# q's product in the last layer's PSUM bank, beside k's in one step

## The chip, the core and the metric

The kernel runs on one core of a Trainium2 chip. Its time is in device microseconds; below it stands as the median of three runs. TensorE does the matmuls, ScalarE and VectorE read their results out of PSUM (GpSimd does the small arithmetic on rows in SBUF), and SyncE issues most DMAs. PSUM is used in eight banks of 128 partitions by 512 fp32.

## The reference

Eight batches of 512 tokens with 128 features go through three residual layers, each on a layer norm of its input:

```python
x = x + 0.5 * ffn(layernorm(x))      # "pre": fc1 128->512, silu, fc2 512->128, residual inside
x = x + attn(layernorm(x))           # 16 heads of 8
x = x + 0.5 * ffn(layernorm(x))      # "post": the same weights as "pre"
```

In the attention, `q, k, v = split(x @ w_qkv)`, `w = relu(q k^T / sqrt(8))`, each row of `w` is divided by its sum plus 1e-6, `out = w v`, then `y = x + out @ w_out + b_out` and a layer norm with gamma and beta. Everything is fp32; the ffn's weights are dequantised in the kernel.

## The kernel before

The attention of a batch b sets the beat. It goes in 16 steps (four groups of four heads, by four tiles of 128 keys). In each step TensorE computes four score products of 512 queries (`step_scores`, line 831, one bank each), ScalarE takes the relu of two of them and VectorE of the other two (lines 1135 and 1408; in some steps ScalarE takes three), and TensorE then computes the values with the probabilities of the step before (`step_values`, line 854, eight matmuls). The scores of a step can be written only when the relus of the step before are done, since the four score banks are single.

All other matmuls are written by hand into gaps of these steps. The lists `PE_START` (batch 0), `PE_SECOND` (batch 1), `PE_ORDER` (batches 2 to 5), `PE_BARE` (batch 6) and `PE_END` (batch 7) name for each step what comes before and behind the values; `ACT_*` and `DVE_*` name what ScalarE and VectorE do behind their relus, in order. An entry as `pre.k@1` is for batch b + 1, `post.fc1.0@-1` for batch b - 1. So in the middle of attention b, the first layer of batches b + 1 and b + 2, the k, q and v of batch b + 1, and the last layer of batches b - 1 and b - 2 are computed.

The first layer and k, q and v go through one PSUM bank, `pre.bank`; the last layer and the output projection `op` go through another, `post.bank`. A fill of a bank is one product group, and each has an eviction. Semaphores count them: `full` goes up when a fill is written and `free` when it is evicted, and `PRE_SEQUENCE` and `POST_SEQUENCE` list the order of the fills, so that `after(fill, b)` gives the count to wait for. `next_fill` makes TensorE wait until the fill before has been evicted.

q and k are kept in two parts: ScalarE copies the rounded high part (line 1049), and VectorE computes the rest from the same bank (line 1242, tasks `q_lo` and `k_lo`), and that sets `free`. SyncE then spreads both into the operands `k_op` and `q_op` (lines 724 and 730), in queue order: the wait for k, k's DMAs, the wait for q, q's DMAs. The u that the three products read comes as a transpose on TensorE (`uT`, batches 0 to 2 and 7) or by VectorE blocks and DMAs (`U_BY_DMA`, batches 3 to 6). Likewise the last layer's h is turned by transposes (`hT`) or, for batches 1 to 4, by a trip through DRAM (`turn`, line 696); fc1's first quarter waits for its four copies back.

Line 762 holds the products by 32 tokens (fc2, v, op), line 769 those by columns (fc1, k, q), line 754 the transposes. In the middle of a batch GpSimd works on the statistics and normalisation of x, the residuals, and v's operand `v_op`.

Of the kernel before, what the change touches and what calls it, by code (L numbers as in the profile page):

```python
# [8 lines left out]
ACT = mybir.ActivationFunctionType  # L9
# [33 lines left out]
def pre_sequence():  # L43

    entries = [(fill, 0) for fill in FIRST_FILLS] + [(fill, 1) for fill in PRE_FILLS[:6]]
    for b in range(1, B):
        split = 4 if b == 1 else 5
        after = [fill for fill in ("uT", "k", "q", "v") if not (fill == "uT" and b in U_BY_DMA)]
        for fills, batch in ((PRE_FILLS[1:split], b + 1), (after, b), (PRE_FILLS[split:6], b + 1)):
            entries += [(fill, batch) for fill in fills if batch < B]  # L50
    return entries
# [1 line left out]

PRE_SEQUENCE = pre_sequence()
PRE_BY_DMA, POST_BY_DMA = range(2, B), range(1, B - 3)
POST_SEQUENCE = [(fill, b) for b in range(B) for fill in POST_FILLS if not (fill == "hT" and b in POST_BY_DMA)]


FIRST_PARTS = [("k0", 0), ("q0", 0), ("q0", 1), ("k0", 1)]
# [35 lines left out]
    ([], ["pre.fc1.3@2"]),  # L95
    ([], ["pre.uT@1"]),
    ([], ["pre.k@1"]),
    ([], ["post.hT@-1", "pre.q@1"]),
    ([], ["pre.v@1"]),
    ([], ["post.fc1.0@-1"]),  # L100
    ([], ["post.fc1.1@-1"]),
    ([], ["post.fc1.2@-1"]),
# [11 lines left out]
    (["pre.fc1.1@2"], []),  # L114
    (["pre.fc1.2@2"], []),
    (["pre.fc1.3@2"], []),
    ([], ["pre.k@1"]),
    ([], ["pre.q@1", "post.fc1.0@-1"]),
    ([], ["post.fc1.1@-1", "pre.v@1"]),
    ([], ["post.fc1.2@-1"]),  # L120
    ([], ["post.fc1.3@-1", "pre.fc2.0@2"]),
]
# [9 lines left out]
    ([], ["pre.uT@1"]),  # L132
    ([], ["pre.k@1"]),
    ([], ["pre.q@1"]),
    ([], ["post.hT@-1", "pre.v@1"]),
    ([], ["post.fc1.0@-1"]),
    ([], ["post.fc1.1@-1"]),
    ([], ["post.fc1.2@-1"]),
# [62 lines left out]
    ["pre.fc1.3@2"],  # L201
    ["pre.uT@1"],
    ["pre.k@1"],
    ["post.hT@-1", "pre.q@1"],
    ["pre.v@1"],
    ["post.fc1.0@-1"],
    ["post.fc1.1@-1"],
    ["post.fc1.2@-1"],
# [11 lines left out]
    ["pre.fc1.1@2"],  # L220
    ["pre.fc1.2@2"],
    ["post.store@-2", "pre.fc1.3@2"],
    ["pre.k@1"],
    ["pre.q@1", "post.fc1.0@-1"],
    ["post.fc1.1@-1", "pre.v@1"],
    ["post.fc1.2@-1"],
    ["post.fc1.3@-1"],
]
# [9 lines left out]
    ["pre.uT@1"],  # L238
    ["post.store@-2", "pre.k@1"],
    ["pre.q@1"],  # L240
    ["post.hT@-1", "pre.v@1"],
    ["post.fc1.0@-1"],
    ["post.fc1.1@-1"],
    ["post.fc1.2@-1"],
# [74 lines left out]
    ["post.out@-2"],  # L319
    ["post.turn@-1"],  # L320
    [],
    ["pre.k_lo@1"],
    ["pre.x_stats@3", "pre.q_lo@1"],
    ["oT.0", "den.0"],
    ["pre.turn@3"],
    ["a.0"],
# [94 lines left out]
def build(nc, x, w_qk, w_v, w_out, fc1_q, fc2_q, fc2_scales, columns, lines, out):  # L421
# [4 lines left out]
    with ExitStack() as ctx:  # L426
# [42 lines left out]
        class Stage:  # L469
# [19 lines left out]

            def base(self, b):  # L490

                return sum(batch < b for _, batch in self.sequence)

            def after(self, fill, b):

# [172 lines left out]
        def _(sp):  # L668
# [32 lines left out]
            def iteration(b):  # L701
                n = b + 1
                if n == 1:
                    turn(pre, 2)
                if n in U_BY_DMA:
                    send(u_by_copies, n)
                    fetch(u_by_copies, n, (pre.full, pre.after("v", b)))
                if b - 1 in post.by_dma:
                    turn(post, b - 1)
                for g in range(NG):  # L710
                    if n > 0 and g == NG - 1 and b + 3 in pre.by_dma:

                        turn(pre, b + 3)
                    if n > 0:
                        sp.wait_ge(scores_done[1], 2 * STEPS * b + 2 * TT * (g + 1))
                    if n == 0 and g == 0:

                        continue
                    if n == 0 and g == 1:
                        sp.wait_ge(*emptied(pre, 1, "k"))  # L720
                    elif g == 0:
                        sp.wait_ge(pre.free, pre.after("k", n))
                    for i in range(2):
                        sp.dma_start(rows_to(k_op, g, i), rows_of(1, slice(0, 2), g)).then_inc(qk_in[g], 16)
                    if n == 0 and g == 1:
                        sp.wait_ge(*emptied(pre, 1, "q"))
                    elif g == 0:
                        sp.wait_ge(pre.free, pre.after("q", n))
                    for i in range(2):
                        sp.dma_start(rows_to(q_op, g, i), rows_of(0, i, g).unsqueeze(1).to_broadcast([ROW, 2, S])  # L730
                                     ).then_inc(qk_in[g], 16)
# [5 lines left out]
        def _(pe):  # L737
# [120 lines left out]
            def task(stage, what, b):  # L858
                if stage == "pre":
                    if what == "uT":  # L860
                        next_fill(pre, b, "uT")
                        transposes(pre, b, u1, u_rows)
                    elif what in ("q", "k"):
                        i = "qk".index(what)
                        next_fill(pre, b, what)
                        if b in U_BY_DMA:
                            pe.wait_ge(u_by_copies.t_in, TURN_DONE * u_by_copies.turns(b))
                        by_columns(pre.bank[:, :], wqk[:, i, :], t_u[:, :]).then_inc(pre.full, 1)
                    elif what == "v":
                        if b in U_BY_DMA:  # L870
                            pe.wait_ge(u_by_copies.t_in, TURN_DONE * u_by_copies.turns(b))
                        else:
                            pe.wait_ge(pre.free, pre.after("uT", b))
                        next_fill(pre, b, "v")
                        for t in range(TT):
                            last = by_tokens(pre.bank, t_u, t, wv[:, :], True, True)
                        last.then_inc(pre.full, 1)
                    else:
                        ffn(pre, b, what)
                elif stage == "post":  # L880
                    if what == "op":
                        if b == 0:
                            pe.wait_ge(wo_loaded, 16)
                        pe.wait_ge(aT_in, b + 1)
                        if b > 0:

                            last_use = "fc2" if b == B - 2 else "fc1.3"
                            pe.wait_ge(post.free, post.after(last_use, b - 1))
                        for t in range(TT):
                            last = by_tokens(post.bank, aT, t, wo[:, :], True, True, b in U_BY_DMA)  # L890
                        last.then_inc(op_done, 1)
                    else:
                        ffn(post, b, what)
# [122 lines left out]
        def _(act):  # L1016
# [20 lines left out]
            def task(stage, what, b):  # L1037
                if stage == "pre":
# [3 lines left out]
                    elif what in ("q", "k"):  # L1042
                        i = "qk".index(what)
                        if what == "k" and b > 0:
                            for g in range(NG):
                                if copied(g, b - 1) > 0:
                                    act.wait_ge(qk_in[g], copied(g, b - 1))
                        act.wait_ge(pre.full, pre.after(what, b))
                        activation(qk_parts[i][:, 0, :], pre.bank[:, :], ACT.Copy, scale=QK_SCALES[i]).then_inc(high_in[i], 1)  # L1049
                    elif what == "v":  # L1050
                        if b > 0:
                            act.wait_ge(v_in, NG * b)
# [88 lines left out]
        def _(dve):  # L1141
# [52 lines left out]
            def task(stage, what, b):  # L1194
# [29 lines left out]
                elif stage == "pre":  # L1224
# [13 lines left out]
                        row_stats(norm_x1, b, x1)  # L1238
                    elif what in ("q_lo", "k_lo"):
                        i = "qk".index(what[0])  # L1240
                        dve.wait_ge(high_in[i], b + 1)
                        v.scalar_tensor_tensor(qk_parts[i][:, 1, :], pre.bank[:, :], QK_SCALES[i],  # L1242
                                               qk_parts[i][:, 0, :].bitcast(F32), ALU.mult, ALU.subtract
                                               ).then_inc(pre.free, 1)
                elif stage == "post":
                    if what == "y":
                        dve.wait_ge(op_done, b + 1)
# [396 lines left out]
```

## Time and profile before

| | |
|---|---|
| median of three runs | 355.91 us (355.38 to 356.16) |
| the profiled execution | 355.84 us |
| its span, first to last instruction | 354.0 us |
| TensorE busy | 344.6 us (97%) |
| VectorE busy | 265.9 us (75%) |
| GpSimd busy | 223.2 us (63%) |
| ScalarE busy | 220.8 us (62%) |

Busy is the time in which an engine has an instruction under way. Matmuls are pipelined and their ends are modelled, so that in the timeline one group's time runs into the next one's start; distances between starts are the safer measure.

### The profile page before, as it was taken

What the parts mean: (1) busy time and instruction counts of PE and PEld (TensorE: products, weight loads), DVE (VectorE), ACT (ScalarE), POOL (GpSimd) and SP (SyncE); (2) the same over time, 40 slices, a digit from 0 to 9 for tenths busy, and PEclk for the clock granted to TensorE, in tenths of its full rate; (3) what the DMA queues carried; (4) which work ended last, traced back from release to release, by engine and by line L of the source; (5) the groups of instructions that cost most, each with busy time, mean ns of one, the idle gap of its engine ahead of it and who ended that gap; (6) DMA issues with size and microseconds to landing.
All of it is one profiled execution on the core that took longest, in us unless ns stands there. A gap on an engine that the chain in (4) does not pass through costs nothing.

```text
span 354.0 us, 12690 instructions
## 1 busy us (share of the span) xinstructions
PE 344.6 (97%) x4946; PEld 152.1 (43%) x4946; DVE 265.9 (75%) x658; ACT 220.8 (62%) x396; POOL 223.2 (63%) x469
## 2 busy tenths in 40 slices
PE   7989999999999999999999999999999999999986
PEld 6732523532345423552346423553245533532365
DVE  4756557875878878887788869997668866678773
ACT  3377477577755667457665677547774577677623
POOL 7588187089864899089962899268941884046441
PEclk9999999999999999999999999999999999999999
DMA  7017105510623046513364035511470026200001
GB/s 215 11 39 175 61 30 130 163 40 5 156 81 96 31 126 151 147 30 112 87 163 122 19 131 126 152 27 56 127 192 22 2 61 150 64 29 1 4 4 61
DMA packets 24187, 30.06 MB, mean 85 GB/s; under 512 B 3648, under 2 KB 12096, under 8 KB 24128
## 3 DMA queue, kind: packets, MB, share of 16 engines
q1 hardware_dynamic: 21536, 25.18, 26.9%
q10 hardware_dynamic: 2592, 4.07, 3.7%
q8 instruction: 40, 0.66, 0.8%
q14 instruction: 19, 0.16, 0.1%
HBM read 7.21 MB, written 5.77 MB: 37 GB/s over the span
## 4 chain that ended last, share of the span: by engine, by line
PE 91%; DVE 3%; ACT 2%; issue 1%; DMA 1%; POOL 1%; ACTq 0%; DVEq 0%
PE o_bank L854 33%; PE scores L831 16%; PE pre_bank L769 11%; PE pre_bank L762 10%; PE post_bank L762 9%; PE post_bank L769 6%; PE scores L769 3%; DVE k_parts L1242 1%; ACT k_parts L1049 1%; DMA pre_x<-in_x_dram 1%; ACT probs L1135 1%; PE pre_bank L754 1%; PE o_bank L748 1%; PE post_bank L754 0%; POOL norm_x_rs L1456 0%
## 5 line engine op out<-in xcount | busy, mean ns | idle before, releaser
L1135 ACT ACTIVATE probs<-scores 128x512 f32<-128x512 f32 x279 | 149.9, 597 | 71.7 <-PE scores L831 69.7
L1408 DVE TENSOR_SCALAR probs<-scores 128x512 f32<-128x512 f32 x220 | 141.7, 679 | 42.9 <-PE scores L831 39.3
L854 PE MATMUL o_bank<-probs,v_op 128*32 128x512 f32 x1024 | 135.7, 602 | 0.8 <-ACT probs L1135 0.4
L831 PE MATMUL scores<-q_op,k_op 32*128 32x512 f32 x499 | 67.1, 495 | 0.4 <-DVE q_op L1344 0.4
L831 PEld LDWEIGHTS scores<-q_op,k_op 32*128 32x128 f32 x499 | 26.2, 181 | 69.8 <-issue 53.8
L1438 POOL TENSOR_SCALAR norm_y_var<-norm_y_mv 128x4 f32<-128x4 f32 x7 | 1.4, 200 | 70.7 <-DVE norm_y_mv L1191 70.7
L854 PEld LDWEIGHTS o_bank<-probs,v_op 128*32 128x32 f32 x1024 | 22.4, 108 | 38.0 <-issue 37.9
L762 PEld LDWEIGHTS post_bank<-w,post_y 128*32 128x32 f32 x960 | 27.1, 110 | 13.6 <-issue 12.7
L762 PEld LDWEIGHTS pre_bank<-w,pre_y 128*32 128x32 f32 x960 | 27.1, 110 | 12.6 <-issue 11.8
L762 PE MATMUL pre_bank<-w,pre_y 128*32 128x128 f32 x960 | 31.6, 273 | 0.0
L762 PE MATMUL post_bank<-w,post_y 128*32 128x128 f32 x960 | 31.0, 273 | 0.0
L769 PE MATMUL pre_bank<-pre_t,w_whole 128*32 128x512 f32 x224 | 29.6, 600 | 0.0
L1034 ACT ACTIVATE post_y<-post_bank,b_sum,col_consts 128x512 f32<-128x512 f32 x24 | 18.7, 779 | 12.7 <-PE post_bank L769 12.7
L1034 ACT ACTIVATE pre_y<-pre_bank,b_sum,col_consts 128x512 f32<-128x512 f32 x28 | 21.8, 779 | 5.7 <-PE pre_bank L769 5.6
L769 PE MATMUL post_bank<-post_t,w_whole 128*32 128x512 f32 x192 | 25.0, 593 | 0.1
L1441 POOL TENSOR_TENSOR norm_x_rs<-norm_x_var,minus_half 128x4 f32<-128x4 f32 x21 | 21.3, 1014 | 1.8
L1511 POOL TENSOR_TENSOR v_op<-v_rows,v_op 128x128 f32<-128x128 f32 (+1 forms) x33 | 13.8, 430 | 6.4 <-ACT v_rows L1054 6.4
L1478 POOL TENSOR_TENSOR norm_x_rs<-norm_x_var,minus_half 128x4 f32<-128x4 f32 x16 | 16.2, 1011 | 1.3
L1438 POOL TENSOR_SCALAR norm_x_var<-norm_x_mv 128x4 f32<-128x4 f32 x21 | 7.2, 344 | 12.9 <-DVE norm_x_mv L1191 11.3
L769 PE MATMUL pre_bank<-t_u,wqk 128*32 128x512 f32 x112 | 14.8, 598 | 0.5
L1494 POOL TENSOR_SCALAR pre_xr<-pre_x,norm_x_mix 128x128 f32<-128x128 f32 x32 | 14.5, 469 | 0.8
L1469 POOL TENSOR_SCALAR u<-x,norm_x_rs,norm_x_shift 128x128 f32<-128x128 f32 x28 | 12.3, 456 | 1.5 <-POOL norm_x_shift L1445 1.2
(175 smaller groups left out, 427.2 us busy)
## 6 DMA issues: line engine op xcount, KB each, us to landing
k_op<-k_parts SPq DMA_DIRECT2D x62, 128.0 KB, 2.7
q_op<-q_parts SPq DMA_DIRECT2D x62, 128.0 KB, 2.7
out_dram<-o_rows ACTq DMA_DIRECT2D x7, 256.0 KB, 2.4
pre_x<-in_x_dram ACTq DMA_DIRECT2D x6, 256.0 KB, 3.0
pre_past<-pre_blocks SPq DMA_DIRECT2D x6, 256.0 KB, 3.2
pre_t<-pre_past SPq DMA_DIRECT2D x24, 64.0 KB, 2.1
u_past<-u_blocks SPq DMA_DIRECT2D x4, 256.0 KB, 2.2
t_u<-u_past SPq DMA_DIRECT2D x16, 64.0 KB, 2.0
```

The source lines that it names most:

```text
L762: last = mm(into[VW * j:VW * (j + 1), P * t:P * (t + 1)], tokens[:, part], w, start=start, stop=stop)
L769: last = mm(into[part, :], w[:, part], tokens, start=True, stop=True)
L831: mm(score_bank(b, s, i, j), k_op[rows, g, P * kt:P * (kt + 1)], q_op[rows, g, :], start=True, stop=True).then_inc(scores_done[i], 1)
L854: last = mm(o_bank[pair][VW * j:VW * (j + 1), :], v_op[:, kt, heads_of(g).start + 2 * j, :], probs[:, s % 2, j, :], start=(odd == 0 and kt ...
L1034: activation(st.y[:, f, :], fc1_bank(st, b, f), ACT.Silu, bias=b1_sum[:, f:f + 1], scale=s1_col[:, f:f + 1]).then_inc(st.free, 1)
L1135: activation(probs[:, s % 2, 2 * i + j, :], score_bank(b, s, i, j), ACT.Relu).then_inc(probs_done[i][j], 1)
L1408: v.tensor_scalar(probs[:, s % 2, 2 * i + j, :], score_bank(b, s, i, j), 0.0, None, ALU.max).then_inc(probs_done[i][j], 1)
L1441: p.tensor_tensor(norm.rs[:, i, :], norm.var[:, i, :], minus_half[:, i, :], ALU.pow).then_inc(norm.rs_in, 1)
L1469: last = p.tensor_scalar(dst[:, t, :], rows[:, t, :], norm.rs[:, i, t:t + 1], norm.shift[:, i, t:t + 1], ALU.mult, ALU.add)
L1478: p.tensor_tensor(norm.rs[:, 0, :], norm.var[:, 0, :], minus_half[:, 0, :], ALU.pow).then_inc(norm.half_in, 1)
L1494: last = p.tensor_scalar(st.xr[:, t, :], st.x(b)[:, t, :], norm.mix[:, 0, t:t + 1], norm.mix[:, 1, t:t + 1], ALU.mult, ALU.add)
L1511: return p.tensor_tensor(v_op[:, ts, heads, first:first + HD], rows, by_one, ALU.mult)
```

## The change

q's product of batches 1 to 7 is written to `post.bank` and evicted from there; k's stays in `pre.bank`. `PRE_SEQUENCE` loses its q fills and `POST_SEQUENCE` gains them, each behind the fc2 of batch b - 2 in the attention of batch b, and ahead of the last layer's fills of batch b - 1. `base` now gives the place of a batch's first fill other than q.

In batches 2 to 5, k and q stand behind the values of step 11, v and fc1's first quarter behind those of step 12, and the second quarter alone behind those of step 13. ScalarE's and VectorE's lists follow; VectorE's statistics of x stay in step 12, where q's rest was. In batches 1 and 6, where k stands in step 9, the last layer's `hT` moves behind v in step 11. Where u comes by transposes, TensorE waits for its copy before q by a wait of its own, and in batch 1 for the first q's eviction. SyncE waits for q on `post.free`.

```diff
--- before.py
+++ after.py
@@ -45,7 +45,7 @@
     entries = [(fill, 0) for fill in FIRST_FILLS] + [(fill, 1) for fill in PRE_FILLS[:6]]
     for b in range(1, B):
         split = 4 if b == 1 else 5
-        after = [fill for fill in ("uT", "k", "q", "v") if not (fill == "uT" and b in U_BY_DMA)]
+        after = [fill for fill in ("uT", "k", "v") if not (fill == "uT" and b in U_BY_DMA)]
         for fills, batch in ((PRE_FILLS[1:split], b + 1), (after, b), (PRE_FILLS[split:6], b + 1)):
             entries += [(fill, batch) for fill in fills if batch < B]
     return entries
@@ -53,7 +53,19 @@
 
 PRE_SEQUENCE = pre_sequence()
 PRE_BY_DMA, POST_BY_DMA = range(2, B), range(1, B - 3)
-POST_SEQUENCE = [(fill, b) for b in range(B) for fill in POST_FILLS if not (fill == "hT" and b in POST_BY_DMA)]
+
+
+def post_sequence():
+
+    entries = [("q", 1)]
+    for b in range(1, B + 1):
+        entries += [("fc2", b - 2)] if b > 1 else []
+        entries += [("q", b + 1)] if b + 1 < B else []
+        entries += [(fill, b - 1) for fill in POST_FILLS[0:5] if not (fill == "hT" and b - 1 in POST_BY_DMA)]
+    return entries + [("fc2", B - 1)]
+
+
+POST_SEQUENCE = post_sequence()
 
 
 FIRST_PARTS = [("k0", 0), ("q0", 0), ("q0", 1), ("k0", 1)]
@@ -95,8 +107,8 @@
     ([], ["pre.fc1.3@2"]),
     ([], ["pre.uT@1"]),
     ([], ["pre.k@1"]),
-    ([], ["post.hT@-1", "pre.q@1"]),
-    ([], ["pre.v@1"]),
+    ([], ["pre.q@1"]),
+    ([], ["pre.v@1", "post.hT@-1"]),
     ([], ["post.fc1.0@-1"]),
     ([], ["post.fc1.1@-1"]),
     ([], ["post.fc1.2@-1"]),
@@ -114,9 +126,9 @@
     (["pre.fc1.1@2"], []),
     (["pre.fc1.2@2"], []),
     (["pre.fc1.3@2"], []),
-    ([], ["pre.k@1"]),
-    ([], ["pre.q@1", "post.fc1.0@-1"]),
-    ([], ["post.fc1.1@-1", "pre.v@1"]),
+    ([], ["pre.k@1", "pre.q@1"]),
+    ([], ["pre.v@1", "post.fc1.0@-1"]),
+    ([], ["post.fc1.1@-1"]),
     ([], ["post.fc1.2@-1"]),
     ([], ["post.fc1.3@-1", "pre.fc2.0@2"]),
 ]
@@ -132,7 +144,7 @@
     ([], ["pre.uT@1"]),
     ([], ["pre.k@1"]),
     ([], ["pre.q@1"]),
-    ([], ["post.hT@-1", "pre.v@1"]),
+    ([], ["pre.v@1", "post.hT@-1"]),
     ([], ["post.fc1.0@-1"]),
     ([], ["post.fc1.1@-1"]),
     ([], ["post.fc1.2@-1"]),
@@ -201,8 +213,8 @@
     ["pre.fc1.3@2"],
     ["pre.uT@1"],
     ["pre.k@1"],
-    ["post.hT@-1", "pre.q@1"],
-    ["pre.v@1"],
+    ["pre.q@1"],
+    ["pre.v@1", "post.hT@-1"],
     ["post.fc1.0@-1"],
     ["post.fc1.1@-1"],
     ["post.fc1.2@-1"],
@@ -220,9 +232,9 @@
     ["pre.fc1.1@2"],
     ["pre.fc1.2@2"],
     ["post.store@-2", "pre.fc1.3@2"],
-    ["pre.k@1"],
-    ["pre.q@1", "post.fc1.0@-1"],
-    ["post.fc1.1@-1", "pre.v@1"],
+    ["pre.k@1", "pre.q@1"],
+    ["pre.v@1", "post.fc1.0@-1"],
+    ["post.fc1.1@-1"],
     ["post.fc1.2@-1"],
     ["post.fc1.3@-1"],
 ]
@@ -238,7 +250,7 @@
     ["pre.uT@1"],
     ["post.store@-2", "pre.k@1"],
     ["pre.q@1"],
-    ["post.hT@-1", "pre.v@1"],
+    ["pre.v@1", "post.hT@-1"],
     ["post.fc1.0@-1"],
     ["post.fc1.1@-1"],
     ["post.fc1.2@-1"],
@@ -319,8 +331,8 @@
     ["post.out@-2"],
     ["post.turn@-1"],
     [],
-    ["pre.k_lo@1"],
-    ["pre.x_stats@3", "pre.q_lo@1"],
+    ["pre.k_lo@1", "pre.q_lo@1"],
+    ["pre.x_stats@3"],
     ["oT.0", "den.0"],
     ["pre.turn@3"],
     ["a.0"],
@@ -489,7 +501,8 @@
 
             def base(self, b):
 
-                return sum(batch < b for _, batch in self.sequence)
+                return min((i for i, (fill, batch) in enumerate(self.sequence) if batch == b and fill != "q"),
+                           default=len(self.sequence))
 
             def after(self, fill, b):
 
@@ -725,7 +738,7 @@
                     if n == 0 and g == 1:
                         sp.wait_ge(*emptied(pre, 1, "q"))
                     elif g == 0:
-                        sp.wait_ge(pre.free, pre.after("q", n))
+                        sp.wait_ge(post.free, post.after("q", n))
                     for i in range(2):
                         sp.dma_start(rows_to(q_op, g, i), rows_of(0, i, g).unsqueeze(1).to_broadcast([ROW, 2, S])
                                      ).then_inc(qk_in[g], 16)
@@ -862,10 +875,14 @@
                         transposes(pre, b, u1, u_rows)
                     elif what in ("q", "k"):
                         i = "qk".index(what)
-                        next_fill(pre, b, what)
+                        st = (post, pre)[i]
+                        next_fill(st, b, what)
                         if b in U_BY_DMA:
                             pe.wait_ge(u_by_copies.t_in, TURN_DONE * u_by_copies.turns(b))
-                        by_columns(pre.bank[:, :], wqk[:, i, :], t_u[:, :]).then_inc(pre.full, 1)
+                        elif what == "q":
+                            pe.wait_ge(pre.free, pre.after("uT", b))
+                            pe.wait_ge(*emptied(pre, 1, "q"))
+                        by_columns(st.bank[:, :], wqk[:, i, :], t_u[:, :]).then_inc(st.full, 1)
                     elif what == "v":
                         if b in U_BY_DMA:
                             pe.wait_ge(u_by_copies.t_in, TURN_DONE * u_by_copies.turns(b))
@@ -1045,8 +1062,9 @@
                             for g in range(NG):
                                 if copied(g, b - 1) > 0:
                                     act.wait_ge(qk_in[g], copied(g, b - 1))
-                        act.wait_ge(pre.full, pre.after(what, b))
-                        activation(qk_parts[i][:, 0, :], pre.bank[:, :], ACT.Copy, scale=QK_SCALES[i]).then_inc(high_in[i], 1)
+                        st = (post, pre)[i]
+                        act.wait_ge(st.full, st.after(what, b))
+                        activation(qk_parts[i][:, 0, :], st.bank[:, :], ACT.Copy, scale=QK_SCALES[i]).then_inc(high_in[i], 1)
                     elif what == "v":
                         if b > 0:
                             act.wait_ge(v_in, NG * b)
@@ -1238,10 +1256,11 @@
                         row_stats(norm_x1, b, x1)
                     elif what in ("q_lo", "k_lo"):
                         i = "qk".index(what[0])
+                        st = (post, pre)[i]
                         dve.wait_ge(high_in[i], b + 1)
-                        v.scalar_tensor_tensor(qk_parts[i][:, 1, :], pre.bank[:, :], QK_SCALES[i],
+                        v.scalar_tensor_tensor(qk_parts[i][:, 1, :], st.bank[:, :], QK_SCALES[i],
                                                qk_parts[i][:, 0, :].bitcast(F32), ALU.mult, ALU.subtract
-                                               ).then_inc(pre.free, 1)
+                                               ).then_inc(st.free, 1)
                 elif stage == "post":
                     if what == "y":
                         dve.wait_ge(op_done, b + 1)
```

## Rows read from the trace of the kernel before

**Rows 1.** The page: busy times (part 1) and one of the costliest groups (part 5).
```profile
PE 344.6 (97%) x4946; PEld 152.1 (43%) x4946; DVE 265.9 (75%) x658; ACT 220.8 (62%) x396; POOL 223.2 (63%) x469
...
L1438 POOL TENSOR_SCALAR norm_y_var<-norm_y_mv 128x4 f32<-128x4 f32 x7 | 1.4, 200 | 70.7 <-DVE norm_y_mv L1191 70.7
```

**Rows 2.** Who waited for line 1242, the second half of k's and q's evictions.
```profile
  PEld pre_bank L769: 6.0, 6
  PEld pre_bank L762: 2.0, 2
```

**Rows 3.** The chain of waits, batch 2, around q: start us, us, what.
```profile
129.83 0.61 ACT k_parts L1049
...
130.46 0.70 DVE k_parts L1242
```

**Rows 4.** Timeline of TensorE, batch 2, steps 11 to 14: start us, us, what.
```profile
127.32 0.51 PE L831 MATMUL scores<-q_op,k_op 32*128 32x512 f32 x4
...
128.64 1.04 PE L769 MATMUL pre_bank<-t_u,wqk 128*32 128x512 f32 x8
129.61 0.50 PE L831 MATMUL scores<-q_op,k_op 32*128 32x512 f32 x4
130.04 1.07 PE L854 MATMUL o_bank<-probs,v_op 128*32 128x512 f32 x8
131.21 1.07 PE L769 MATMUL pre_bank<-t_u,wqk 128*32 128x512 f32 x8
132.32 1.06 PE L769 MATMUL post_bank<-post_t,w_whole 128*32 128x512 f32 x8
...
136.48 0.50 PE L831 MATMUL scores<-q_op,k_op 32*128 32x512 f32 x4
```

**Rows 5.** Timeline of TensorE, batches 3 and 4: q's product, then fc1's first quarter.
```profile
171.96 1.07 PE L769 MATMUL pre_bank<-t_u,wqk 128*32 128x512 f32 x8
173.07 1.06 PE L769 MATMUL post_bank<-post_t,w_whole 128*32 128x512 f32 x8
...
212.74 1.07 PE L769 MATMUL pre_bank<-t_u,wqk 128*32 128x512 f32 x8
213.62 1.04 PE L769 MATMUL post_bank<-post_t,w_whole 128*32 128x512 f32 x8
```

**Rows 6.** The four DMAs that fetch batch 2's turned h for fc1, read in batch 3.
```profile
DMA to landing us min/median/max: 1.8/2.2/3.5
```

**Rows 7.** Timeline of TensorE, batch 6: values, then hT's transposes.
```profile
290.00 1.06 PE L854 MATMUL o_bank<-probs,v_op 128*32 128x512 f32 x8
291.00 0.66 PE L754 MATMUL post_bank<-ident,post_h 128*128 128x128 f32 x4
```

**Rows 8.** Timeline of VectorE, batch 2, step 12 to the next batch's step 0.
```profile
131.07 1.28 DVE L1408 TENSOR_SCALAR probs<-scores 128x512 f32<-128x512 f32 x2
132.26 0.86 DVE L1182 BATCH_NORM_STATS2 norm_x_stats<-pre_x 128x6 f32<-128x128 f32 x4
...
133.46 0.66 DVE L1242 SCALAR_TENSOR_TENSOR q_parts<-pre_bank,q_parts 128x512 fp32r<-128x512 f32 x1
...
135.22 0.70 DVE L1200 STREAM_TRANSPOSE o_t<-o_bank 128x512 f32<-128x512 f32 x1
...
136.20 0.35 DVE L1205 RECIPROCAL rec<-den 128x32 f32<-128x32 f32 x1
137.12 1.29 DVE L1408 TENSOR_SCALAR probs<-scores 128x512 f32<-128x512 f32 x2 [0.56 <-PE scores L831]
...
140.60 1.65 DVE L1210 TENSOR_TENSOR a_t<-o_t,rec 128x256 f32<-128x256 f32 x1
142.57 1.29 DVE L1408 TENSOR_SCALAR probs<-scores 128x512 f32<-128x512 f32 x2 [0.32 <-PE scores L831]
```

**Rows 9.** Timeline of GpSimd, batch 2: x's statistics taken up; v_op.
```profile
134.55 0.20 POOL L1438 TENSOR_SCALAR norm_x_var<-norm_x_mv 128x4 f32<-128x4 f32 x1
...
141.54 0.43 POOL L1511 TENSOR_TENSOR v_op<-v_rows,v_op 128x128 f32<-128x128 f32 x1
```

## The prediction

> **What bounds the kernel now.** I read the page's busy times first: TensorE is busy for 344.6 of 354.0 us [rows 1]. A gain has to make TensorE's stream shorter or take a hole out of it, and here even the 3% without work understates the holes, since a matmul's modelled end runs on over a wait. So I looked for holes where the change works, at q's evictions. The list of who waits for the second half of a k or q eviction (line 1242) names TensorE's weight loads eight times: six times a q or k product, and twice v's [rows 2]. The chain of waits shows one of them in batch 2 as a detour off TensorE: ScalarE's copy at 129.83, VectorE's rest from 130.46 to 131.16, then q's product at 131.21 [rows 3, 4].
>
> The timeline of that stretch gives the prices [rows 4]. A group of 8 matmuls behind another takes 0.88 us (212.74 to 213.62) [rows 5]. Behind the values at 130.04 q should have begun at 130.92 and began at 131.21: **0.29 us** of hole. And fc1's first quarter, 0.88 behind q's start where nothing is late (the same pair of batch 4), came 1.11 behind it in batches 2 and 3 (131.21 to 132.32, 171.96 to 173.07) [rows 4, 5]: **0.23 us** more.
>
> Of that 0.23 I take the cause to be the turned h, which fc1 waits for. In batch 3 the last of its four copies lands up to 3.5 us after its issue [rows 6], and the others in 1.8 to 2.2. It arrives some 5.0 us after the scores of step 11 (132.32 less 127.32), and fc1 was up by then.
>
> **The change, part by part.** The instructions stay the same in number, form and size: no matmul, no copy, no DMA is added or removed. What moves:
>
> *q in the other bank.* q's product no longer waits for k's eviction, and v's no longer for q's. In batches 2 to 5 k, q and the scores follow each other; in batches 0, 1 and 6 q stays a step behind k. All eight waits go: six of q on k (batches 0 and 2 to 6) and two of v on q (batches 0 and 1). 8 x 0.29 = **2.32 us**. Each lies on the path, as TensorE has no slack behind it.
>
> *The order in step 12.* Now fc1's first quarter comes behind v. With the scores of step 11 at T, the new stream is: values T+0.43, k T+1.32, q T+2.20, scores T+3.17, values T+3.60, v T+4.48, fc1.0 T+5.36, scores T+6.33 (the values come 0.43 behind the scores, 129.61 to 130.04, a group 0.88 behind another, and the scores 0.97 behind a group, 128.64 to 129.61: [rows 4, 5]). fc1.0 comes 0.36 us behind the landing at T+5.0, so both 0.23 go as well: **0.46 us**. That margin is the cover; if a copy lands 0.5 us later, 0.13 comes back per batch.
>
> *hT behind v.* In batches 1 and 6, TensorE now goes values, v, hT, scores in place of values, hT, q or v, scores. A change from 32-column products to whole-array transposes costs 0.12 (1.00 from values to hT, 290.00 to 291.00, against 0.88) [rows 7], and leaving it costs as much before the next 32-column group. hT just ahead of the scores saves one of the two by my reading, as the scores pay for leaving the 32-column form anyhow. 2 x 0.12 = **0.24 us**, an estimate; its bounds are 0 and 0.24.
>
> *New waits on the post bank.* q's turn needs the bank free of the y product and of the last out: the out is taken in step 8, two steps or more before q (steps 10 to 12), so this wait ends long before. fc1.0 (or hT) needs q's eviction. ScalarE starts 1.19 us after a product's start (k at 128.64, copy at 129.83) [rows 3, 4], so q's copy starts at T+3.39 and VectorE's rest at T+4.02, which ends at T+4.7; fc1.0 is up at T+5.36. v needs k's, which ended at T+3.84 (131.16) against T+4.48. Nothing is late. SyncE's queue gets the q wait earlier and has the same DMAs; q's operand is used a batch later.
>
> *What queues behind the two evictions.* Here is the cost. VectorE now does k_lo, q_lo and then the relu of step 12; behind it the statistics of x, the relu of step 13, and oT, den and rec. Its pitches are 0.61 for a rest (130.46 to 131.07), 1.19 for two relus (131.07 to 132.26), 1.20 for the statistics (132.26 to 133.46) and 1.33 for oT to rec (135.22 to 136.55) [rows 3, 8]. From T+4.02: relu 12 at T+4.63, statistics T+5.82, relu 13 T+7.02 to 8.31 (its scores, at T+6.33, can be read 0.64 later: 136.48 to 137.12 [rows 4, 8]). Scores of step 13 need relu 12, which ends at T+5.92, and come at T+6.33; those of step 14 need T+8.31 and come at T+8.61. Then oT from T+8.21 to 9.54, relu 14 to T+10.83, with the scores of step 15 at T+10.89. That is 0.01 of room after 0.05 for the hand-over (131.16 to 131.21). GpSimd takes up the statistics at T+7.23 (134.55) [rows 9]; they are ready at T+7.10, so its chain and the turn of h behind it stay put.
>
> One thing does not shorten: a_t ran 1.65 us, from 140.60 to 142.25, and ended 0.28 after GpSimd's three two-input operations (v_op to 141.97) [rows 8, 9]. I take GpSimd's timing as fixed, so a_t ends again at T+14.93. The next batch's scores come at T+14.05 and could be read at T+14.69, so the relu begins 0.24 late. Before, VectorE waited 0.32 at this place [rows 8]. The relu ends at T+16.22, and the next scores come at T+16.33. So again nearly free, at most 0.2 in each of batches 2, 3 and 4, which have statistics and this a_t. Bounds 0 and 3 x 0.2 = 0.6; with rooms that come out positive by hundredths I take **0.15 us** for the three.
>
> Two relus of 0.68 us take 1.29 together and the next operation starts 1.19 after the first [rows 8]: VectorE overlaps the tail of one with the next, and the sum goes by that. The Trainium skill, VectorE: DVE Perf Modes, "The DRAIN you can't avoid", speaks against so tight a queue: it has each VectorE operation followed by a flush of about its time less 266 ns before the next issues, unless the next is one that starts earlier. By its figures the two relus would take about 1.8 us, relu 12 would end some 1.2 us later, and an estimate from that page is a time about 0.6 us above before, on the side of rival C. The trace shows the overlap, so the page's case does not apply here.
>
> **Sum.** 2.32 + 0.46 + 0.24 - 0.15 = 2.87 us. The profiled execution took 355.84 us around its span of 354.0, and the median is 355.91, so the two are one number. 355.84 - 2.87 = **352.97, say 353.0 us**, a span of 351.1.
>
> **The rivals.**
> *A: VectorE's queue gives part back.* For: 0.01 us of room at step 15's scores, and the late a_t. Against: VectorE idled 0.56 us before relu 14 and 0.32 before the next batch's first, which is what the shorter steps draw on [rows 8]. If a_t or den meets GpSimd differently, or fc1's copies land late, some 0.4 us is lost in each of batches 2, 3, 4, over my sum: 353.0 + 1.2 = 354.2 us. It decides once the queue is 0.1 us later than I have it.
> *B: no change.* A ring other than TensorE sets a batch's period, such as GpSimd's chain from y's statistics to the next turn. Against this, GpSimd stood idle 70.7 us in seven waits for those statistics [rows 1], 10 us a batch. Or q finds the post bank taken: the out would have to be 6 us late. All is given back: 355.8 us.
> *C: slower.* The relu of step 12, queued behind two evictions, holds up the scores of step 13. The scores move once relu 12 ends 0.36 us later than T+5.92. For it: a_t shows that VectorE can be held beside GpSimd's work, 1.65 us for an operation of 128x256 [rows 8], and the two rests now run together while GpSimd works. Held like that, k_lo and q_lo would each take 1.65 in place of 0.69, relu 12 would end 1.92 later and the scores move 1.92 - 0.36 = 1.56 us in each of batches 2 to 5. Their gain is 2 x 0.52 + 2 x 0.29 = 1.62, that of batches 0, 1 and 6 is 4 x 0.29 + 0.24 = 1.4: 4 x 1.56 - 3.02 = 3.2 slower, 359.0 us. The sign turns when the scores move 0.76 in each, relu 12 ending 1.1 late. Against: q's rest took 0.66 and the relus behind it kept their pitch [rows 8].
>
> **How the numbers follow.** Forecast 0.67, A 0.20, B 0.08, C 0.05. The forecast's own bounds are 355.84 - 3.02 = 352.8 (no lateness) and 355.84 - 2.32 - 0.46 + 0.6 = 353.7 (no saving at hT, all the lateness); the runs shown lie within 0.8 of each other. The range reaches into A: 352.4 to 354.4. Within 0.2% of before, about what a measurement here can tell, is 355.2 to 356.6. So faster is the forecast, A and a little of B, 0.88; same 0.07; slower 0.05.
>
> **What the changed profile would show.** Right: the waits for line 1242's evictions gone from the weight loads; batches 2 and 3 from step 11's scores to step 14's in 8.61 us in place of 9.16; k and q 0.88 apart; batch 0's steps 12 and 13 at 2.3 us. Wrong: scores in steps 13 to 15 or at the start of the next batch waiting for VectorE's relu; fc1.0 more than 0.9 behind v; hT to scores costing 0.7 or more. The prediction falls if the stream after step 13 is spaced by VectorE and not by TensorE.

## The result, and the profile after

| | before | after |
|---|---|---|
| median, 6 runs each | 355.65 us (355.38 to 356.16) | **353.78 us** (353.35 to 353.96) |
| the profiled execution | 355.84 us | 353.96 us |
| its span | 354.0 us | 352.0 us |

The ratio is 0.9944, with a 95% interval of 0.9931 to 0.9957: 1.87 us faster, where I had forecast 2.87. Every profiled execution of before and after has a granted clock of 1.00. Of all executions of the other kernels one is left out of the ratios: 362.58 us at a granted clock of 0.95, in experiment 6. The page's busy times after, beside [rows 1]:

```profile
PE 343.4 (98%) x4946; PEld 153.8 (44%) x4946; DVE 267.1 (76%) x658; ACT 220.6 (63%) x396; POOL 221.7 (63%) x469
```

The counts are the same. The second halves of the evictions (now line 1261), with who waited for them:

```profile
L1261 DVE SCALAR_TENSOR_TENSOR k_parts<-pre_bank,k_parts x7: 692/692/693, 53.4 to 285.7; 128x512 fp32r<-128x512 f32 x7
L1261 DVE SCALAR_TENSOR_TENSOR q_parts<-post_bank,q_parts x7: 691/691/692, 55.6 to 287.9; 128x512 fp32r<-128x512 f32 x7
...
who waited for it (us, times):
busy tenths in 40 slices 0000001000000010000100000000100010000000
```

The list is empty where [rows 2] had eight waits. TensorE in batch 2, steps 11 to 14, beside [rows 4]:

```profile
126.74 0.51 PE L844 MATMUL scores<-q_op,k_op 32*128 32x512 f32 x4
127.17 1.07 PE L867 MATMUL o_bank<-probs,v_op 128*32 128x512 f32 x8
128.06 1.04 PE L782 MATMUL pre_bank<-t_u,wqk 128*32 128x512 f32 x8
128.91 1.04 PE L782 MATMUL post_bank<-t_u,wqk 128*32 128x512 f32 x8
129.88 0.51 PE L844 MATMUL scores<-q_op,k_op 32*128 32x512 f32 x4
...
131.21 1.06 PE L775 MATMUL pre_bank<-wv,t_u 128*32 128x128 f32 x32
132.08 1.04 PE L782 MATMUL post_bank<-post_t,w_whole 128*32 128x512 f32 x8
133.05 0.50 PE L844 MATMUL scores<-q_op,k_op 32*128 32x512 f32 x4
...
135.34 0.51 PE L844 MATMUL scores<-q_op,k_op 32*128 32x512 f32 x4
```

k and q are 0.85 apart, fc1's first quarter is 0.87 behind v, and scores 11 to scores 14 take 8.60 us where I forecast 8.61. The stream in batch 2 is the one of the prediction. So is VectorE's queue, beside [rows 8]: relu 12 starts 4.52 us behind the scores of step 11 (forecast 4.63), relu 13 at 6.95 (7.02), and a_t ends at 14.85 (14.93).

```profile
130.65 0.69 DVE L1261 SCALAR_TENSOR_TENSOR q_parts<-post_bank,q_parts 128x512 fp32r<-128x512 f32 x1
131.26 1.28 DVE L1427 TENSOR_SCALAR probs<-scores 128x512 f32<-128x512 f32 x2
132.46 0.86 DVE L1200 BATCH_NORM_STATS2 norm_x_stats<-pre_x 128x6 f32<-128x128 f32 x4
...
133.69 1.29 DVE L1427 TENSOR_SCALAR probs<-scores 128x512 f32<-128x512 f32 x2
...
139.50 2.09 DVE L1228 TENSOR_TENSOR a_t<-o_t,rec 128x256 f32<-128x256 f32 x1
```

To find the missing 1 us I measured every batch by the distance from its first scores to the next batch's first scores (batch 7: to its last), in each trace. Two more traces of before and one more of after were taken for it (the last three experiments below):

| us | b0 | b1 | b2 | b3 | b4 | b5 | b6 | b7 | sum |
|---|---|---|---|---|---|---|---|---|---|
| before, profiled | 40.49 | 39.22 | 40.77 | 40.75 | 40.53 | 40.49 | 38.06 | 28.27 | 308.58 |
| before, second trace | 40.45 | 39.24 | 40.50 | 40.52 | 40.53 | 40.49 | 38.06 | 28.25 | 308.04 |
| before, third trace | 40.48 | 39.21 | 40.52 | 40.53 | 40.49 | 40.51 | 38.03 | 28.26 | 308.03 |
| after, profiled | 39.89 | 38.80 | 40.20 | 40.22 | 40.36 | 40.20 | 38.28 | 28.25 | 306.20 |
| after, second trace | 39.89 | 38.82 | 40.21 | 40.20 | 40.37 | 40.20 | 38.29 | 28.26 | 306.24 |
| gain, first of after against second of before | 0.56 | 0.44 | 0.30 | 0.30 | 0.17 | 0.29 | **-0.22** | 0.00 | 1.84 |

The two traces of after agree within 0.02 in each batch. Two things stand out. Batches 2 and 3 of the one trace that I had are some 0.25 us longer than in the other two: that loss is not in every execution. And batch 6 got slower. The place in it, by all engines of after, steps 12 to 14:

```profile
289.66 0.60 ACT L1072 ACTIVATE v_rows<-pre_bank 128x512 f32<-128x512 f32 x1 [0.33 <-PE pre_bank L775]
...
290.34 0.81 POOL L1530 TENSOR_TENSOR v_op<-v_rows,v_op 128x128 f32<-128x128 f32 x2 [0.76 <-ACT v_rows L1072]
...
291.11 1.29 POOL L1585 TENSOR_TENSOR u_bias<-u,rows 128x512 f32<-128x512 f32 x1
...
292.35 1.28 POOL L1575 TENSOR_TENSOR x_beta<-x,rows 128x512 f32<-128x512 f32 x1
...
292.64 1.05 DVE L1221 TENSOR_TENSOR den<-o_t,kern_eps 128x32 f32<-128x32 f32 x1
...
293.99 1.22 DVE L1427 TENSOR_SCALAR probs<-scores 128x512 f32<-128x512 f32 x2
294.63 0.23 PEld L844 LDWEIGHTS scores<-q_op,k_op 32*128 32x128 f32 x3 [0.84 <-ACT probs L1153]
294.63 1.14 PE L844 MATMUL scores<-q_op,k_op 32*128 32x512 f32 x4
...
295.27 0.18 PEld L844 LDWEIGHTS scores<-q_op,k_op 32*128 32x128 f32 x1 [0.41 <-DVE probs L1427]
295.69 0.16 PEld L867 LDWEIGHTS o_bank<-probs,v_op 128*32 128x32 f32 x8 [0.24 <-issue]
```

Read it from the end. The fourth score product of step 14 waits for VectorE's relu of step 13: the values behind it come 1.06 us after the scores, not 0.43, and the step takes 2.92 us, not 2.29. The relu began at 293.99 because `den`, an addition of 128x32, ran from 292.64 to 293.69, 1.05 us. It is 0.21 us in batch 2. GpSimd's `x_beta` ran over it, 292.35 to 293.63. The same stretch of before, in its second trace:

```profile
292.39 0.60 ACT L1054 ACTIVATE v_rows<-pre_bank 128x512 f32<-128x512 f32 x1 [0.50 <-PE pre_bank L762]
...
293.84 1.28 POOL L1566 TENSOR_TENSOR u_bias<-u,rows 128x512 f32<-128x512 f32 x1
...
294.77 0.40 DVE L1203 TENSOR_TENSOR den<-o_t,kern_eps 128x32 f32<-128x32 f32 x1
...
295.08 1.29 POOL L1556 TENSOR_TENSOR x_beta<-x,rows 128x512 f32<-128x512 f32 x1
```

There `den` met the seam between the two sums and was through in 0.40 us. The change takes v ahead of `hT`, so v's rows are copied before the step begins and not behind its start. GpSimd starts its chain of v's operand and the two sums earlier against the scores, and the second sum, not the seam, lies over `den`.

### The profile page after: what moved, and what is told of

Same layout as the page of the kernel before. It is cut to its first block, busy times and chain, and to the rows that moved or that the text cites. A ratio compares the mean times of both kernels' runs of the same rounds, so it can differ in the third digit from the quotient of the medians.

```text
span 352.0 us, 12693 instructions
## 1 busy us (share of the span) xinstructions
PE 343.4 (98%) x4946; PEld 153.8 (44%) x4946; DVE 267.1 (76%) x658; ACT 220.6 (63%) x396; POOL 221.7 (63%) x469
## 4 chain that ended last, share of the span: by engine, by line
PE 91%; DVE 3%; DMA 2%; ACT 1%; issue 1%; SPq 0%; DVEq 0%; ACTq 0%
PE o_bank L867 34%; PE scores L844 16%; PE pre_bank L775 10%; PE pre_bank L782 9%; PE post_bank L775 9%; PE post_bank L782 7%; PE scores L782 2%; DMA s_rows<-in_L_ffn_fc_scales_dram 2%; ACT probs L1153 1%; PE pre_bank L767 1%; PE o_bank L761 1%; DVE probs L1427 1%; PE post_bank L767 1%; DVE post_x L1391 0%; DVE den L1221 0%
## 5 line engine op out<-in xcount | busy, mean ns | idle before, releaser
L1488 POOL TENSOR_SCALAR pre_h<-pre_x,norm_x_rs,norm_x_shift 128x128 f32<-128x128 f32 x28 | 12.3, 450 | 1.3 <-POOL norm_x_shift L1464 1.3
```

Source lines behind the costliest of these rows:

```text
L1488: last = p.tensor_scalar(dst[:, t, :], rows[:, t, :], norm.rs[:, i, t:t + 1], norm.shift[:, i, t:t + 1], ALU.mult, ALU.add)
```

## The experiments

Medians stand beside those of before on the same chip (355.66 for the first four, 355.71 for the next four, 355.58 for the last four).

**1. `den` a step later, in batch 6 alone** (in VectorE's list of batch 6):

```diff
-    ["oT.0", "den.0"],
-    ["a.0"],
+    ["oT.0"],
+    ["den.0", "a.0"],
```

> The changed kernel (353.78 us) with one thing moved: in batch 6, VectorE's den and rec go from step 12 to step 13, behind that step's relu. Theory (GpSimd holds den): in the changed kernel's trace den took 1.05 us there instead of about 0.21 to 0.39, beside GpSimd's two-input sums, so relu 13 was late and the scores of step 14 came 2.92 us behind those of step 13 instead of 2.29. With den out of the way: 2.29 again, 0.63 us less, 353.15 us. Rival 1 (ScalarE's three relus in steps 10 and 11 are late): nothing changes, 353.8. Rival 2 (VectorE's queue is too long as it is, held or not): also 353.15, so this run tells only rival 1 apart.

Measured: 353.37 us (352.89 to 353.91), ratio 0.9934 [0.9923, 0.9945]. The interval overlaps that of after (0.9931 to 0.9957), so it is the trace that tells the gain: step 14 of batch 6 takes 2.29 us again and the batch 37.68. (The gap meant in the expectation is the one from scores 14 to scores 15; it names it one step early.)

```profile
292.68 1.29 DVE L1427 TENSOR_SCALAR probs<-scores 128x512 f32<-128x512 f32 x2 [0.37 <-PE scores L844]
293.89 0.20 DVE L1221 TENSOR_TENSOR den<-o_t,kern_eps 128x32 f32<-128x32 f32 x1
```

`den` behind the relu takes 0.20 us and the step's 0.63 is back. It doesn't say yet whether the long `den` or the mere length of VectorE's list was the cause.

**2. GpSimd's two sums out of `den`'s way**, VectorE's lists as in after (batch 6's sums go to batch 7):

```diff
-                work(b, POOL_ORDER)
+                order = POOL_ORDER
+                if b == B - 2:
+                    order = POOL_ORDER[:-2]
+                elif b == B - 1:
+                    order = POOL_ORDER[:3] + ["post.u_bias", "pre.x1_beta"] + POOL_ORDER[3:]
+                work(b, order)
```

> The changed kernel with VectorE's lists as they are; instead GpSimd's two sums of batch 7 (u plus bias, x1 plus beta, 1.3 us each) go from the end of its list of batch 6 to behind y_gamma in its list of batch 7. Theory (GpSimd holds den): den takes 0.2 to 0.4 us, step 13 to step 14 of batch 6 is 2.29 us, 353.15 us. Rival (VectorE's queue is too long even if nothing holds it): 2.9 us stays, 353.8.

Measured: 353.73 us (353.38 to 354.28), ratio 0.9945 [0.9933, 0.9957].

```profile
292.47 0.71 DVE L1218 STREAM_TRANSPOSE o_t<-o_bank 128x512 f32<-128x512 f32 x1
293.21 0.21 DVE L1221 TENSOR_TENSOR den<-o_t,kern_eps 128x32 f32<-128x32 f32 x1
...
317.53 1.29 POOL L1585 TENSOR_TENSOR u_bias<-u,rows 128x512 f32<-128x512 f32 x1
...
317.60 1.77 DVE L1280 TENSOR_TENSOR post_x<-y_rows,x_beta 128x512 f32<-128x512 f32 x1
...
318.77 1.74 POOL L1575 TENSOR_TENSOR x_beta<-x,rows 128x512 f32<-128x512 f32 x1
```

With VectorE's list unchanged `den` is 0.21 us and the step 2.29: GpSimd's sums are the cause. The time didn't follow, since the sums now meet another two-input operation of VectorE in batch 7, whose length goes from 28.25 to 28.74. The wait is not removed but moved. (This trace also has one late DMA in batch 2, 0.55 us that no other trace has.)

**3. `hT` ahead of v in batches 1 and 6**, as in before, with q's bank as in after:

```diff
-    ([], ["pre.v@1", "post.hT@-1"]),
+    ([], ["post.hT@-1", "pre.v@1"]),
```

(and the same in ScalarE's lists, and for batch 6)

> The changed kernel with hT ahead of v again in step 11 of batches 1 and 6, on TensorE and ScalarE. It prices the order: by my sum hT last saves 0.12 us in each, so step 11 goes from 2.92 to 3.03 us in both, 0.22 slower. And v later moves GpSimd's sums some 0.6 us later against den: if den is held only while one of them runs, it now meets the seam between the two and is let through sooner, step 13 to 14 of batch 6 goes back to 2.3 to 2.4 us: 353.4 us in all. Rival (the queue is too long, held or not): 2.92 there, 354.0 us.

Measured: 353.61 us (353.09 to 353.99), ratio 0.9944 [0.993, 0.9959]. Step 11 takes 3.11 in both batches, not 2.92: the order is worth 0.19 us each. But ScalarE copies v's rows 0.20 us behind the scores of step 12 again (290.06 against 289.86; in before's second trace 292.39 against 292.19), and not 0.39 ahead of them, as in after (289.66 against 290.05). `den` meets the seam, and step 14 takes 2.3 us:

```profile
291.50 1.28 POOL L1585 TENSOR_TENSOR u_bias<-u,rows 128x512 f32<-128x512 f32 x1
...
292.44 0.40 DVE L1221 TENSOR_TENSOR den<-o_t,kern_eps 128x32 f32<-128x32 f32 x1
...
292.73 1.31 POOL L1575 TENSOR_TENSOR x_beta<-x,rows 128x512 f32<-128x512 f32 x1
```

So the place of v alone turns `den`'s long wait on or off.

**4. `den` later in batch 6, and the statistics ahead of the two evictions in batches 2 to 4**, against batch 4's lateness:

```diff
-    ["pre.k_lo@1", "pre.q_lo@1"],
-    ["pre.x_stats@3"],
+    ["pre.x_stats@3", "pre.k_lo@1", "pre.q_lo@1"],
+    [],
```

> The changed kernel with den of batch 6 in step 13 and, in batches 2 to 5, the statistics of x at the head of VectorE's step 11 instead of behind relu 12. VectorE idled 1.2 us in step 11 until ScalarE's copy of k, and the statistics take 1.20. Theory: the 0.63 us of batch 6 and the 0.13 us of batch 4 (steps 14 and 15 of 2.32 and 3.27 us) come back: 353.0 us. Rival: the statistics run over into k's rest and v is late by as much, up to 0.1 us in each of three batches: 353.3.

Measured: 353.30 us (353.05 to 353.99), ratio 0.9938 [0.9926, 0.995]. Batch 6 as in the first experiment, batch 4 still 0.13 longer. **5. The statistics alone**, the same edit without `den`'s:

> The changed kernel with the statistics of x at the head of VectorE's step 11 in batches 2 to 5, where it idled 1.2 us before k's rest. Theory: batch 4's steps 14 and 15 go from 2.32 and 3.27 back to 2.29 and 3.16, 0.13 us, nothing else moves: 353.65 us. Rival (the queue behind the two evictions costs more than the trace shows, also in batches 2 and 3): up to 0.5 us less, 353.3. Batch 6 keeps its 2.92.

Measured: 353.97 us (353.4 to 354.86), ratio 0.9952 [0.9939, 0.9965]. Batch 4 is 40.35 as in after. With the statistics gone VectorE idles 1.51 us ahead of relu 13 of batch 4, and it still starts 0.99 us behind its scores, where 0.64 is usual. The theory that VectorE's queue makes that relu late falls.

**6. fc1's first quarter ahead of v** in batches 2 to 5:

```diff
-    ([], ["pre.v@1", "post.fc1.0@-1"]),
+    ([], ["post.fc1.0@-1", "pre.v@1"]),
```

> The changed kernel with fc1's first quarter ahead of v in step 12 of batches 2 to 5. It would start at T+4.48 (T: scores of step 11), but q's eviction ends at T+4.70 and, in batches 2 and 3, the turned h lands at about T+5.0 by my reading. Theory: steps 12 to 13 become 3.17 + 0.27 = 3.44 us in batches 4 and 5 and 3.17 + 0.5 = 3.7 us in batches 2 and 3: 1.5 us slower than the changed kernel, 355.3 us. Rival (the 0.23 us of batches 2 and 3 in the kernel before was no landing but a restart behind q's wait): 3.44 in all four, 354.9 us.

Measured: 355.15 us over ten runs (354.10 to 356.92 without the one of 362.58), ratio 0.999 [0.9973, 1.0006] by the nine. Step 12 takes 3.38 us in all four batches against 3.17. Who waited for line 1261:

```profile
  PEld post_bank L782: 3.7, 4
```

The new wait is for q's eviction, which fc1's bank needs. It costs 0.21 in each, 0.9 together, where I had expected 1.5; the median is 1.4 above after's, and what makes the rest is open, so that it lies near the 355.3 I had expected is no support for the theory. It didn't tell a late landing of the turned h from no landing wait, as the eviction ended last in all four.

**7. The new order alone**: before, with k and q in one step and v and fc1.0 in the next, in batches 2 to 5, and q still in k's bank.

```diff
-    ([], ["pre.k@1"]),
-    ([], ["pre.q@1", "post.fc1.0@-1"]),
-    ([], ["post.fc1.1@-1", "pre.v@1"]),
+    ([], ["pre.k@1", "pre.q@1"]),
+    ([], ["pre.v@1", "post.fc1.0@-1"]),
+    ([], ["post.fc1.1@-1"]),
```

> The kernel before, one bank for k and q as it was, but with the new order of batches 2 to 5 (k and q in step 11, v and fc1's first quarter in step 12). Theory: q waits for k's eviction, until T+3.89 in place of T+2.20, and v another 0.2 us for q's, so step 11 to step 14 takes about 10.5 us in place of 9.16 and 8.90: 6 us slower than before, about 361.7 us. Rival (the order brings the gain, the bank little): no slower than 355.7.

Measured: 363.17 us, one execution. q waits for the whole of k's eviction, and v for q's:

```profile
131.60 1.06 PE L769 MATMUL pre_bank<-t_u,wqk 128*32 128x512 f32 x8 [1.52 <-DVE k_parts L1242]
```

**8. The new bank alone**: after, with before's order in batches 2 to 5 (the diff above the other way).

> The changed kernel, q in the last layer's bank, but with the order of before in batches 2 to 5 (k in step 11, q and fc1's first quarter in step 12, v in step 13). Batches 0, 1 and 6 as in the changed kernel. Theory: fc1's first quarter now waits for q's eviction, which stands behind relu 12 and the statistics on VectorE and ends at T+6.9, so fc1 starts about 2.0 us later than in the kernel before in each of four batches, 8 us in all; batches 0, 1 and 6 keep their 0.8 us: about 363 us. Rival (the bank brings the gain, the order little): 354 us.

Measured: 364.98 us, one execution, at a mean granted clock of 0.99. fc1's first quarter stands right behind q in the same bank and waits:

```profile
132.83 1.07 PE L782 MATMUL post_bank<-post_t,w_whole 128*32 128x512 f32 x8 [2.19 <-DVE q_parts L1261]
```

Not all of the 9.3 us above before is that wait. In batches 3 and 4, behind waits of 2.20 and 2.19 us, TensorE's granted clock falls to 0.50 (its lower level, 1.2 of 2.4 GHz) from 176 to 178 us and from 221 to 223 us, the group of the values takes 1.94 us in place of 1.06, and step 13 takes 4.39 and 4.59 us in place of 3.17: 2.6 us of the total. Behind the wait of batch 2, 2.19 us as well, the clock stays at 1.00 and step 13 takes 3.17.

Each half by itself costs 7.5 or 9.3 us. The bank gives the gain and the order keeps the bank from taking it back.

**9. `den` a step later in all of batches 2 to 6**: the first experiment's edit, and in VectorE's list of batches 2 to 5

```diff
-    ["oT.0", "den.0"],
-    ["pre.turn@3"],
+    ["oT.0"],
+    ["den.0", "pre.turn@3"],
```

> The kernel with den of batch 6 a step later, and in batches 2 to 5 too den and rec go from step 13 to step 14, ahead of the turn of h. In batch 4 the relu of step 13 began 0.99 us behind its scores in the kernel before and in every changed one, also where VectorE stood idle ahead of it, against 0.64 elsewhere; so oT, den and rec ran late into relu 14. Theory: with 0.6 us less ahead of relu 14, batch 4's steps 14 and 15 are 2.29 and 3.16 us again (they were 2.32 and 3.27), 0.13 us less than with den moved in batch 6 alone: 353.25 us. Rival (the late relu 13 moves on as it is, or den now meets GpSimd's two-input work): no gain, or a step 15 longer than 3.27.

Measured: **352.82 us** (352.35 to 353.74), ratio 0.9929 [0.9915, 0.9942], the fastest of all; by the ratios 0.5 us below after, with intervals that still overlap, so that here too the trace tells it. Batch 4 is 40.23, 0.13 shorter than after, batch 6 37.65, 0.63 shorter, and the stretch from first to last scores 305.48, 0.72 shorter. Relu 13 of batch 4 still starts late, but relu 14 no longer stands behind `den` and `rec`:

```profile
213.63 1.29 DVE L1427 TENSOR_SCALAR probs<-scores 128x512 f32<-128x512 f32 x2 [0.31 <-issue]
214.83 0.70 DVE L1218 STREAM_TRANSPOSE o_t<-o_bank 128x512 f32<-128x512 f32 x1
215.56 1.29 DVE L1427 TENSOR_SCALAR probs<-scores 128x512 f32<-128x512 f32 x2
216.77 0.20 DVE L1221 TENSOR_TENSOR den<-o_t,kern_eps 128x32 f32<-128x32 f32 x1
```

**10 to 12. Before twice more and after once more**, unchanged, for a second and third trace.

> The kernel before, unchanged, for a second trace. By the traces the change takes 2.4 us between the first and the last step of attention and by the medians 1.9. Theory (run to run differences in the weights' DMAs at the start): the first scores of the kernel before begin between 21.1 and 21.9 us, as those of the changed kernels, and it was the changed kernel's profiled execution that began late (21.89 against 21.45). Rival (a start that the change makes later): near 21.3 again. And if fc1's 0.23 us of batches 2 and 3 comes from the landing of the turned h, it follows the landing: 3.70 us in step 12 where the last copy lands after T+4.7, 3.45 where it lands sooner.

> The kernel before once more, for a third trace: the same two questions. Step 12 of batches 2 and 3 is 3.70 or 3.45 us with the landing, and the first scores begin anywhere from 21.1 to 21.9 us.

> The changed kernel once more, for a second trace: batch 6's step 13 to 14 of 2.92 us and batch 4's 2.32 and 3.27 us recur, since they are in the order of the work, while the first scores begin elsewhere than at 21.89 us. Rival for both: chance, then they are gone.

Measured: 355.35, 355.76 and 354.30 us. Their batches stand in the table above. Second trace of before, q to fc1 in batch 2, beside [rows 4]:

```profile
131.29 1.06 PE L769 MATMUL pre_bank<-t_u,wqk 128*32 128x512 f32 x8
132.17 1.04 PE L769 MATMUL post_bank<-post_t,w_whole 128*32 128x512 f32 x8
```

0.88, not 1.11. Batch 2's length confirms it: 40.50 and 40.52, not 40.77.

## Why the prediction was right, and what was mis-sized

The mechanism was right and the time fell inside the range; the size was 1 us too large. The measured 353.78 us lies just beyond the bounds that I gave the forecast itself (352.8 to 353.7) and inside the range because that reached into rival A. Point by point:

*The eight waits, 2.32 us: right.* Batch 0 had two of them and is 0.58 shorter by the mean of the two later traces of before. Batches 2, 3 and 5 had one each and are 0.29 to 0.31 shorter.

*`hT` behind v, 0.24 us: right.* Batch 1 is 0.42 shorter: 0.13 for the order, if v's wait is put at 0.29 (steps 10 and 11 took 3.01 + 2.61, now 2.29 + 2.92). In the new stream the other order costs 0.19, by experiment 3.

*The order in step 12, 0.46 us: mis-sized, worth nothing in the median.* I took 0.23 of hole in each of batches 2 and 3 from one execution as if each had it. The second and third traces have it in neither. The cause was as I took it: by the landing events of the traces the last copy of h landed at 132.23 and 172.98, 0.09 us before fc1 began in each of the two batches (132.32 and 173.07), and later than fc1 could have begun 0.88 behind q (132.09 and 172.84). In the other two traces it landed 0.26 to 1.30 us before fc1 began, and there is no hole. What I had wrong is that it happens each time. A sign that it was a chance stood in [rows 6]: 1.8 to 3.5 us for the same DMA.

*That one execution stood for the median: wrong in its parts.* It lay near the median by its total, 355.84 us, with two batches 0.25 too long. Its first scores started at 21.45 us; other traces, before and after alike, have 21.05 to 22.20. The total hid a part that was not typical behind one that happened to be short.

*VectorE's lateness, 0.15 us in batches 2 to 4: about right in sum, not in its place.* Batches 2 and 3 lose nothing. Batch 4 loses 0.13, at relus 13 and 14 and not at a_t. Why relu 13 starts 0.35 late there isn't settled: in after 0.31 us of idle time ahead of it stand under issue, and in experiment 5, 1.51 us under the scores. It is not what before shows in the same place: there the relu also starts 0.99 behind its scores, but q's rest runs right ahead of it, and in batches 2 and 3 of before's second trace it is 0.97 for the same reason. Experiment 9's expectation takes the two for one.

*Batch 6, costed at the gain of a wait and an order (0.29 + 0.12): the step that failed.* It gained those and lost 0.63, so -0.22. I wrote that I take GpSimd's timing as fixed, and that a held operation would cost in batches 2, 3 and 4. Where v is moved, GpSimd's chain behind v is moved too, and I had not followed it in the batch whose `den` lies near it. It showed in a sign that I had named as one of being wrong, scores of steps 13 to 15 waiting for VectorE's relu. This is rival A's mechanism ("if a_t or den meets GpSimd differently"), in one batch that A didn't name.

The sum with these sizes is 2.32 + 0.24 - 0.13 - 0.63 = 1.80, against 1.84 by the traces and 1.87 by the medians.

*Rival B fell*: no other ring set the period, as batches 0 to 5 all got shorter. *Rival C fell*: the two evictions ran in 0.69 us each while GpSimd worked (130.65 above, beside its `norm_x_mix` and `post_xr`, which are no TENSOR_TENSOR). Two relus still take 1.28 to 1.29 us and the statistics follow 1.20 behind, so the flush of the Trainium skill, VectorE: DVE Perf Modes, "The DRAIN you can't avoid", doesn't show in these pitches either, and a time above before did not come. (My 0.6 us for it was also a wrong sum: relu 12 late by 1.2 gives 4 x (1.2 - 0.36) - 3.02 = 0.3 by rival C's own working.)

For `den` a page does bear on the cause: the Trainium skill, GPSIMD Engine Reference, "Key points", says that GpSimd shares its SBUF interfaces with VectorE and that they contend when the VectorE instruction has two SBUF inputs. The traces agree: `den`, with two, takes 0.20 or 0.21 us alone, 0.40 where the first sum ends 0.34 to 0.35 us after it starts, and 1.05 under `x_beta`.

## What to carry to other kernels

A move that only reorders one engine's stream also shifts the engines fed by it: follow each moved product to its reader and on to what that reader does next, in every batch, and look which operation of a third engine then lies beneath. Read a hole in more than one execution before you book it as a gain; the total can be typical while its parts are not. And a second bank and the order that suits it are one change: either alone cost over 7 us here, in one execution each.

## What the runs showed of the hardware

A VectorE operation with two SBUF inputs, begun while GpSimd runs one with two inputs, mostly ends after the GpSimd operation: `den` (0.20 us alone) at 293.69 after `x_beta`'s 293.63, and at 295.17 after `u_bias`'s 295.12 in before's second trace. A larger one ends later: `a_t` of batch 2 of after (128x256, 0.41 us elsewhere) ran from 139.50 to 141.59, under three such operations of which the last, `v_op`, ended at 141.31, and `post_x` (128x512, 0.69 us elsewhere) ended 0.55 us after `u_bias`.

Where two such GpSimd operations follow each other, `den` slipped through at the seam, so its cost depends on when it starts: 0.40 or 1.05 us for 0.20 us of work. `a_t` mostly did not: in batches 2 to 4 of after it took 2.08 or 2.09 us across two seams, but in batch 2 of experiment 9, begun 0.17 us before `u_bias` ended, 0.46 us. What decides it isn't shown. GpSimd is held in turn: `x_beta` took 1.47 us there and 1.74 us beside `post_x`, and not 1.28.

A hole in TensorE's work can cost more than its length: of the three waits of 2.2 us in experiment 8, two were followed by some 2 us at the lower clock, and the third was not.
